# Two gathers in flight at most: every row gather of a DeepFM/CIN kernel waits for the second one ahead of it

## What is computed

```python
emb = embed_table[f_ix, x_idx]                       # 2048 x 26 x 16
lin1 = w1_table[f_ix, x_idx].sum(axis=1, keepdims=True) + w1_bias
s = emb.sum(axis=1)
fm = 0.5 * ((s * s).sum(-1) - (emb * emb).sum(axis=(1, 2)))[:, None]
h = emb.reshape(n, F * D)
h = jax.nn.relu(h @ mlp_w1 + mlp_b1)
h = jax.nn.relu(h @ mlp_w2 + mlp_b2)
mlp_out = h @ mlp_w3 + mlp_b3
x0 = emb.transpose(0, 2, 1)
last = x0
for W in (cin_w0, cin_w1, cin_w2):
    last = jnp.einsum('ndl,ndf,klf->ndk', last, x0, W)
    feats.append(last)
cin_result = jnp.concatenate(feats, axis=-1).sum(axis=1) @ lin_w + lin_b
return lin1 + fm + mlp_out + cin_result
```

## Time and profile before

| | |
|---|---|
| median of 3 runs | 512.74 us (511.46 to 513.53) |
| span of the profiled execution | 694.2 us |
| mean granted TensorE clock | 0.863 |
| busy: PE, PE's weight loads, DVE | 510.3, 415.1, 412.8 us |
| busy: ACT, POOL | 389.0, 356.6 us |
| gathers (L500) | 360, 990 ns each on the mean |
| DMA traffic | 15.57 MB, of it 3.16 MB by the gathers |

### The profile page before, as it was taken

The page is one execution under the profiler, slowest core; times in us unless marked ns, Lnnn a source line. Parts: engine busy times, 40 slices in busy tenths (PEclk is TensorE's granted clock), DMA queues, the critical chain, the costliest instruction groups (busy, mean ns, idle before and its releaser), DMA issues.

```text
span 694.2 us, 6825 instructions
## 1 busy us (share of the span) xinstructions
PE 510.3 (74%) x2235; PEld 415.1 (60%) x2235; DVE 412.8 (59%) x680; ACT 389.0 (56%) x759; POOL 356.6 (51%) x365
## 2 busy tenths in 40 slices
PE   2897918824696959588695959596886949599988
PEld 2865705723484838476574747475765737478666
DVE  6431227903475748376584847484765848478866
ACT  0321628604464847376574847484665748378875
POOL 6665666774465464637466454547374664510000
PEclk9995666975896979979798989899797979899999
DMA  8836434221111111202111111112021111100000
GB/s 176 163 21 117 88 62 103 7 7 5 5 6 7 4 6 4 7 4 8 5 6 5 5 6 6 6 4 8 3 9 5 6 5 5 6 3 1 0 1 0
DMA packets 21508, 15.57 MB, mean 22 GB/s; under 512 B 12790, under 2 KB 19811, under 8 KB 21347
## 3 DMA queue, kind: packets, MB, share of 16 engines
q0 software_dynamic: 11520, 3.16, 13.5%
q1 hardware_dynamic: 6949, 9.99, 5.9%
q10 hardware_dynamic: 3005, 2.01, 1.4%
HBM read 14.92 MB, written 0.21 MB: 22 GB/s over the span
## 4 chain that ended last, share of the span: by engine, by line
PE 28%; DVE 24%; another core or an unknown queue 18%; ACT 15%; issue 11%; DMA 3%; SPq 0%; DVEq 0%
DVE z_lo L803 5%; ACT ps_s L598 5%; ACT z_hi L591 4%; PE ps_y L1197 4%; PE ps_y L1198 3%; DVE ps_y L946 3%; DVE one_hot L935 3%; PE ps_s L1097 2%; DMA w_space<-cin_w 2%; DVE sums L829 2%; PE ps_q L1111 2%; ACT room_a L597 2%; DVE ps_q L814 2%; DVE emb L950 2%
## 5 line engine op out<-in xcount | busy, mean ns | idle before, releaser
L500 POOL DMA_INDIRECT emb<-rows,idx_raw x360 | 356.3, 990 | 253.7 <-issue 101.4
L803 DVE TENSOR_TENSOR z_lo<-ps_s,z_hi 128x512 fp32r<-128x512 f32 (+1 forms) x192 | 132.1, 688 | 138.9 <-ACT ps_s L598 87.6
L591 ACT ACTIVATE z_hi<-ps_s 128x512 fp32r<-128x512 f32 (+1 forms) x192 | 114.2, 595 | 171.9 <-remote 105.6
L1197 PE MATMUL ps_y<-look_hi,one_hot 128*128 128x442 f32 x224 | 92.6, 413 | 91.4 <-DVE one_hot L935 89.6
L598 ACT ACTIVATE ps_s<-ps_s 128x512 f32<-128x512 f32 (+1 forms) x192 | 113.5, 591 | 0.7
L1111 PE MATMUL ps_q<-z_lo,zw_hi 128*127 128x512 f32 (+1 forms) x192 | 86.9, 453 | 32.6 <-DVE z_lo L803 21.1
L1197 PEld LDWEIGHTS ps_y<-look_hi,one_hot 128*128 128x128 f32 x224 | 49.5, 221 | 101.0 <-DVE emb L950 57.1
L1198 PE MATMUL ps_y<-look_lo,one_hot 128*128 128x442 f32 x224 | 89.3, 400 | 0.0
L946 DVE SCALAR_TENSOR_TENSOR ps_y<-tables,look_place,ps_y 128x442 f32<-128x442 f32 x56 | 37.9, 677 | 78.6 <-remote 70.6
L1097 PE MATMUL ps_s<-xt,pick 128*128 128x512 f32 (+1 forms) x192 | 77.1, 414 | 8.6 <-ACT x L582 5.4
L1113 PE MATMUL ps_q<-z_hi,zw_hi 128*127 128x512 f32 (+1 forms) x192 | 78.9, 411 | 0.0
(11 more groups left out here) (191 smaller groups left out, 765.0 us busy)
## 6 DMA issues: line engine op xcount, KB each, us to landing
emb<-rows,idx_raw POOLq DMA_INDIRECT x360
w_space<-rows SPq DMA_DIRECT2D x2, 728.9 KB
m_space<-rows SPq DMA_DIRECT2D x2, 728.9 KB
w_space<-key_scratch SPq DMA_DIRECT2D x1, 1408.0 KB
w<-cin_w SPq DMA_DIRECT2D x2, 416.0 KB, 4.8
w<-cin_w ACTq DMA_DIRECT2D x2, 416.0 KB, 7.6
w_space<-cin_w SPq DMA_DIRECT2D x2, 416.0 KB
w_space<-cin_w ACTq DMA_DIRECT2D x2, 416.0 KB
```

The lines of the kernel that those rows point to most:

```text
L500: pool.indirect_dma_start(emb[t % EMB][:, f, :], None, rows, bass.IndirectOffsetOnAxis(row_ix[:, t, f:f + 1], 0)).then_inc(gathered[t] if ...
L591: act.activation(z_hi[0:k, c, :], ps[0:k, :], ACT.Square)
L803: z = dve.tensor_tensor(z_lo[0:k, u % NC, :], ps, z_hi[0:k, u % NC, :].bitcast(F32), ALU.subtract)
L1197: pe.matmul(o, one_hot[n % 2][:, j, :], look_hi[i][:, ws], start=(j == 0), stop=False)
```

## The change

The 17 semaphores that counted the landings per tile go. In their place stands a ring of four, `landed[0..3]`: gather number n, counted over all tiles, adds to `landed[n % 4]` when it lands. Each gather from the third on waits ahead of its issue until gather n - 2 has landed. ACT's copies, which waited on one semaphore, now wait on all four, for the last four gathers of their tile. No instruction is moved, and all gathers are issued in the same order as before.

```diff
+LANDINGS = 4
+IN_FLIGHT = 2
...
-        gathered = [sem(f"gathered{t}") for t in range(T)]
-        gathered_late = sem("gathered_late")
+        landed = [sem(f"landed{i}") for i in range(LANDINGS)]
...
+        def gather_no(t, f):
+
+            return sum(F - looks(s) for s in range(t)) + f
+
+        def wait_landed(eng, n):
+
+            eng.wait_ge(landed[n % LANDINGS], 16 * (n // LANDINGS + 1))
+
+        def wait_landed_all(eng, n):
+
+            for i in range(LANDINGS):
+                wait_landed(eng, n - i)
...
                         behind = s_no(t - EMB, NC + f // PER_UNIT - 1) if t >= EMB else s_no(0, f // PER_UNIT)
                         pool.wait_ge(hi_ready, behind + 1)
+                    n = gather_no(t, f)
+                    if n >= IN_FLIGHT:
+                        wait_landed(pool, n - IN_FLIGHT)
                     pool.indirect_dma_start(emb[t % EMB][:, f, :], None, rows,
                                             bass.IndirectOffsetOnAxis(row_ix[:, t, f:f + 1], 0)
-                                            ).then_inc(gathered[t] if t < T - 1 or f < EARLY else gathered_late, 16)
+                                            ).then_inc(landed[n % LANDINGS], 16)
...
-                act.wait_ge(gathered[T - 1], 16 * EARLY)
+                wait_landed_all(act, gather_no(T - 1, EARLY) - 1)
...
-                act.wait_ge(gathered_late, 16 * (F - LOOKS - EARLY))
+                wait_landed_all(act, gather_no(T - 1, F - LOOKS) - 1)
...
-                act.wait_ge(gathered[t], 16 * (F - looks(t)))
+                wait_landed_all(act, gather_no(t, F - looks(t)) - 1)
```

## The result

The changed kernel takes 742.58 us (median of 4 runs, 740.48 to 743.91) against 512.1 us: a ratio of 1.452, 95% interval 1.448 to 1.456. The forecast was 582 us with a range of 525 to 640: the direction was right, the size far off.

What follows compares the result with a forecast made beforehand. PE and DVE were taken to set some 27 us per tile, with POOL almost the bound. Gather 53's start at 96 + 450 for 308 gathers + 1.7 + 0.3 + 32.8 made 581, given as 582 us, range 525 to 640.

Steps and rivals of the forecast that it cites:

- What bounds the kernel now: Main loop before the change: PE and DVE set some 27 us per tile, POOL's gathers need 27.5 us.
- holes: Idle stretches of DVE and ACT in the first profile's tiles, 6.9 us in the one shown; forecast absent from the runs.
- The wait of each gather: POOL's gathers, each waiting for the one two ahead: pitch 1.46 us against 1.25, bounds 1.31 to 1.66.
- The landing behind the instruction's end: Time from the end of a gather's instruction to its landing: taken as 1.7 us, bounds 1.4 to 2.1.
- The wake-up: POOL's delay from semaphore to gather start: 0.27 us, read from a gather waiting for ACT; a second wait counted as hidden.
- the sum with the slowest landing in its bounds: Whole kernel with a landing of 2.1 us, pitch 1.66: 96 + 511 + 35 = 642 us.
- The setup: Gathers before the main loop land slowly and queue less: setup ends some 7 us later, gather 53 near 96 instead of 85.09.
- 5 us per pair: Setup, first 16 gathers: lag per pair 5 us instead of 2.5, so the 17th starts near 34 us instead of 26.9.
- ACT's four waits for one: ACT's copies, 17 places, 51 more waits: at most some 0.3 us each, 15 us in all; taken as nothing.
- Faster: Rival: holes exist in the runs and thinner gather traffic ends them, 21 us back over 13 tiles, 492 us; chance 0.05.
- Much slower: Rival: semaphore's way adds in full and wake-up from a landing is longer; pitch over 1.66, 645 to 670 us; chance 0.08.
- No change: Rival: each gather's wait is hidden by a landing of under 1.28 us; 510 to 515 us; chance 0.07.

Runs made afterwards that it cites:

- the second profile: The unchanged kernel before, run and profiled once more: 511.45 us, profiled span 509.6 us.
- the two edits to the kernel before that relieve POOL: Kernel before with two of 22 gathers per tile left out from tile 3 on: 510.33 us, ratio 0.996; kernel before without hi_ready waits: 511.13 us, ratio 1.001.

## Why the prediction was wrong

*What bounds the kernel now: right.* 27 us per tile set by PE and DVE in the runs, no holes: the second profile shows 27.40, and the two edits to the kernel before that relieve POOL gain 0.4% and nothing. That POOL is almost the bound was right too, and all that follows from it: ACT's copies wait, and the time follows POOL's pitch.

*The wait of each gather: here it failed.* The prediction put the pitch at (0.95 + 1.7 + 0.27) / 2 = 1.46 us; it is (706.1 - 123.7) / 307 = 1.90. Two terms were too small. The landing behind the instruction's end: 1.7 was the end of the packets; from issue to landing it is 3.0 us, 2.1 behind the instruction's end. I had written that no row shows the semaphore's part and then set it to nothing, on the ground that recording the packets might slow the profiled execution. Nothing here bears that out: the profiled execution of the changed kernel took 742.15 us, amid its runs' 740.48 to 743.91. The prediction's upper bound of 2.1 us behind the instruction's end was the true landing. The missing part, 0.38 with a landing of 3.02 us and packets until 1.70, makes 0.38 / 2 x 307 = 58 us. The wake-up: 0.27 came from a gather that waits for one semaphore; half of the gathers of the changed kernel wait for two, and start 0.75 us after the landing. I saw the second wait and called it hidden. It isn't: that is 0.49 / 2 x 307 = 75 us, and taking it out of 140 gathers gives 64 back (the pitch without it is 1.69 us, not the 1.64 of the sum). Together 133 us of the 161 us by which the forecast missed (by the pitches themselves, 307 x 0.44, it is 135); even the sum with the slowest landing in its bounds, 642 us, left the wake-up at 0.27.

*The setup: right in its mechanism, too small.* Forecast for the 17th, 26th and 53rd gather: 34, 50 to 55, 96 us; measured 46.0, 61.1, 123.7. The assumption of 5 us per pair was good: the eight pairs ahead of the 17th gather took 5.3 us on the mean, 9.0, 8.2 and 6.4 the first three. But eight pairs of 5 us behind the first gather at 3.84 make 44 us and not the 34 that the prediction wrote down; 10 us of the error are a slip of its arithmetic. The rest comes mostly from later transfers of the setup, which hit single landings again: the chain of the changed kernel has these among its longest pieces (start, us).

```profile
3.83 8.78 DMA emb<-rows,idx_raw
12.87 7.88 DMA emb<-rows,idx_raw
21.02 6.16 DMA emb<-rows,idx_raw
...
70.28 7.77 DMA emb<-rows,idx_raw
...
91.25 7.53 DMA emb<-rows,idx_raw
...
102.90 7.58 DMA emb<-rows,idx_raw
```

The 53rd gather starts 28 us later than forecast: 12 of them are there at the 17th gather already, 16 are added behind it, in which the pitch has its part as well. 582 + 135 + 28 makes 745, against 742.6 measured.

*ACT's four waits for one:* none of the runs isolates them. In the kernel with four in flight they are in place, and its loss of 14.5 us is accounted for by the setup and the pitch.

*The rivals.* "Faster" rested on a tie between bursts of gathers and late semaphores. The second profile of before has the same bursts and no holes, so the bursts alone do not make the holes; why that one execution has them stays open. "Much slower" named the two causes that decided, the semaphore's way and the wake-up, but ended at 670 us. "No change" needed a landing within 1.28 us of the instruction's end; it came 2.1 behind it. The rule of the Trainium skill ("DMA: Bandwidth & Descriptors", section "Anatomy of one DMA") gives about 2.0 us in all for a DMA issued from GpSimd; these gathers of 128 rows take 3.0 us from issue to landing, so the rule is too small for them.

Of what the prediction looked for in the profile, the pairs, the durations of 0.94 us and ACT's waits in every full copy came as named. The pitch lay outside 1.4 to 1.7. Idle time is ended by a DMA 180 times and not some 350, since the second gather of a pair hardly waits. The profile puts 27 of POOL's waits, 39.8 us in all, down to ACT (L591 and L615); but all 27 gathers start 3.68 to 3.94 us after the gather two ahead, as those that wait for the landing do.

Left open: why a second wait costs 0.49 us. The 140 extra instructions fit a wait carried by an instruction of its own; that POOL begins to take up the gather only after that one is my reading, and no view of the profile shows it.

## What to carry to other kernels

A limit of k transfers in flight sets a pitch of (issue to landing + wake-up) / k; compare it with the issuing engine's own pitch. Allow for landings that come late: an engine with no time in hand doesn't make them good, and here even four in flight, one more than the sum asks for, lost 2.8%. Measure the landing at the semaphore, not at the last packet. Count the waits on each instruction: one more, even one long satisfied, can lengthen the wake-up of a chain.

## What the runs showed of the hardware

A gather of 128 rows of 68 bytes from POOL is busy for 0.94 us and lands 3.0 us after its start (medians); the packets end some 0.3 to 0.4 us earlier than that. With the DMA engines full of weights single gathers land after up to 8.8 us (8.8, 7.9 and 6.2 in the chain of the changed kernel from 3.8 to 27 us). POOL starts a gather 0.26 us after the landing it waits for when that is its only wait, and 0.75 us after it when it has a second one, even if that one was satisfied long before (678.7 against 743.66 us for the whole program).
